# Two 3x3 convolutions re-laid: row taps in the partitions, column phase in the free dimension, copies by DMA in groups, half matmuls for half-zero weights, and one layer-norm step moved to VectorE

## The reference, cut to what matters

```python
q = ln(q.reshape(B_, E, L).transpose(0, 2, 1), gq, bq)   # the same for k and v
...
y = xr + conv3(jax.nn.gelu(conv3(xr, c1w, c1b), approximate=False), c2w, c2b)
x = x + y            # x of the sum is the input; xr comes from the normalised image
```

## Time and profile before

| | |
|---|---|
| median of 3 runs | 831.84 us (830.34 to 832.01) |
| the profiled execution: its own time | 833.53 us |
| its span, first to last instruction | 831.7 us |
| PE busy / DVE busy / ACT busy / POOL busy | 90% / 79% / 73% / 59% |
| granted PE clock, mean over the span | 0.995 of full speed (2.4 GHz) |

### The profile page before, as it was taken

One profiled execution on the slowest core, in us unless ns is written; L12 is line 12 of the kernel. 1 busy time (PEld: TensorE's weight loads), 2 busy tenths in 40 slices (PEclk: granted clock), 3 DMA queues, 4 the chain that ended last, 5 costly groups with the idle time before them and its releaser, 6 DMA issues.

```text
span 831.7 us, 18390 instructions
## 1 busy us (share of the span) xinstructions
PE 749.4 (90%) x5704; PEld 536.1 (64%) x5704; DVE 659.3 (79%) x2141; ACT 603.8 (73%) x1287; POOL 491.9 (59%) x1041
## 2 busy tenths in 40 slices
PE   0479999989899999999899999998989999999988
PEld 0257777767456677766656677776645677776753
DVE  5548888987868888888867888898776888887575
ACT  1388888877567888886737888877747788887840
POOL 5356776763346777765436776775335677776410
PEclk9999999999999999999999999999999999999999
DMA  7111160100112132100111216100011213000002
GB/s 256 58 30 30 31 230 5 53 2 1 58 64 90 36 120 111 58 1 1 59 39 52 71 30 230 58 2 1 7 52 65 96 30 130 0 1 1 2 1 101
DMA packets 17643, 47.00 MB, mean 57 GB/s; under 512 B 2080, under 2 KB 2720, under 8 KB 17568
## 3 DMA queue, kind: packets, MB, share of 16 engines
q1 hardware_dynamic: 17568, 46.09, 16.2%
HBM read 37.69 MB, written 8.39 MB: 55 GB/s over the span
## 4 chain that ended last, share of the span: by engine, by line
PE 46%; DVE 23%; issue 11%; POOL 10%; ACT 9%; DMA 1%; DVEq 0%; SPq 0%; ACTq 0%; POOLq 0%
PE y_ps L1011 11%; PE o_bank L1090 6%; PE s_ps L1065 4%; PE pt_ps L1078 4%; POOL ln_rs L724 4%; DVE h_lo L506 3%; DVE ln_st L542 3%; PE ox_ps L1034 3%; DVE h_hi L503 3%; PE s_ps L1124 3%; ACT qk_n L856 3%; PE ox_ps L1124 3%; PE o_bank L1124 3%; PE pt_ps L1124 3%; PE t_ps L1045 2%
## 5 line engine op out<-in xcount | busy, mean ns | idle before, releaser
L856 ACT ACTIVATE qk_n<-y_ps,ln_nr,ln_rs 128x128 f32<-128x128 f32 x256 | 103.7, 459 | 94.7 <-POOL ln_nr L727 94.0
L737 POOL TENSOR_TENSOR sc<-sc,mx 128x512 f32<-128x512 f32 x128 | 133.7, 1045 | 39.2 <-DVE mx L577 39.2
L1011 PE MATMUL y_ps<-w_hi,x_hi 128*128 128x192 f16 (+1 forms) x512 | 148.4, 290 | 0.0
L1011 PE MATMUL y_ps<-w_hi,x_lo 128*128 128x192 f16 (+1 forms) x512 | 148.1, 289 | 0.0
L1011 PE MATMUL y_ps<-w_lo,x_hi 128*128 128x192 f16 (+1 forms) x512 | 148.0, 289 | 0.0
L562 DVE TENSOR_TENSOR sc<-s_ps,biasS 128x512 f32<-128x512 f32 x128 | 86.8, 678 | 54.9 <-PE s_ps L1065 53.7
L1090 PE MATMUL o_bank<-v_bd,pt 128*128 128x66 f32 x1024 | 129.3, 269 | 0.0
L1090 PEld LDWEIGHTS o_bank<-v_bd,pt 128*128 128x128 f32 x1024 | 125.2, 193 | 0.2
L542 DVE BATCH_NORM_STATS2 ln_st<-y_ps 128x6 f32<-128x128 f32 x384 | 88.9, 287 | 42.9 <-PE y_ps L1011 41.1
L720 POOL TENSOR_TENSOR ln_ve<-ln_mv,eps_y 128x3 f32<-128x3 f32 x128 | 33.8, 264 | 148.2 <-DVE ln_mv L547 148.0
L724 POOL TENSOR_TENSOR ln_rs<-ln_ve,neg_half 128x3 f32<-128x3 f32 x128 | 113.3, 885 | 10.7
(11 more groups left out here) (181 smaller groups left out, 1612.4 us busy)
## 6 DMA issues: line engine op xcount, KB each, us to landing
xs<-in_x_sh_dram SPq DMA_DIRECT2D x32, 576.0 KB, 4.2
xst<-in_x_al_dram SPq DMA_DIRECT2D x16, 512.0 KB, 8.0
xf<-in_x_al_dram SPq DMA_DIRECT2D x32, 256.0 KB, 5.3
out_dram<-xf SPq DMA_DIRECT2D x32, 256.0 KB, 2.0
wst<-in_wqkv_dram SPq DMA_DIRECT2D x1, 768.0 KB, 4.2
w1s<-in_w_dram SPq DMA_DIRECT2D x1, 256.0 KB, 8.8
w2s<-in_w_dram SPq DMA_DIRECT2D x1, 256.0 KB, 8.8
biasS<-in_bias_t_dram SPq DMA_DIRECT2D x1, 256.0 KB, 9.7
```

The lines of the kernel that those rows point to most:

```text
L737: pool.tensor_tensor(sc[i % 4][:, :, :, :], sc[i % 4][:, :, :, :], mx[i % 2][:, :, :].unsqueeze(2).to_broadcast([P, HP, TOK, 2]), ALU.subt ...
L856: ins = act.activation(qk_n[j][:, t, :].rearrange("p (h y x) -> p h y x", h=HEADS, y=2), by_head(y_ps[j][:, E * t:E * (t + 1)]), ACT.Identity,
L1011: ins = pe.matmul(y.rearrange("p (t e) -> p t e", t=3)[:, :, cols], xx[r % 2][:, s, a % 2, 2 * TS * (a // 2):2 * TS * (a // 2 + TS)], ww[: ...
```

## The change

- The input of both convolutions now lies in one buffer `x4`: partition = (tap row `ay`, row phase, channel), so each partition group of 64 holds the image shifted by 0 or 1 row, which makes four image rows lie in the partitions; the column phase is in the free dimension. ACT, POOL and DVE write hi and lo parts into small staging buffers (`xr_st`, `h_st`), and SP copies them into `x4` with four DMAs for each group (`place_x`: 5 groups of an image, `place_h`: 7 groups).
- With this layout two of the four taps have non-zero weights for all 128 outputs, and each of the other two for only 64 of them. A tile takes 6 matmuls with 128 output columns and 6 with 64, the two halves alternating. The number of matmuls stays 12.
- `border` is gone: the staging rows carry a zero column, written once, and two memsets on the first and on the last tile's `hst` make the zero rows. The first row of `x4` is cleared after c2 tile 0.
- New order in step -4: c2 tiles 0 and 1, then c1 tiles 11 and 12 (on PE, ACT and DVE); c1 tile 11 uses another bank. DVE does `low` of tile 10 before the head.
- c1 waits for the copies (`x_in`), c2 for its groups of copies (`h_in`), `split` and `low` wait until the staging buffer they write has been copied out.
- In the layer norm the mean is negated by DVE right after the statistics, where POOL did it between variance and power.
- The host lays data and weights out to match.

The diff, cut to its core:

```diff
-        xr_hi = sb("xr_hi", [P, G + 2, G + 2], F16)
-        xr_lo = sb("xr_lo", [P, G + 2, G + 2], F16)
-        hst = [sb(f"hst{i}", [P, T1R, G + 1]) for i in range(6)]
-        h_hi = sb("h_hi", [P, G + 1, G + 1], F16)
-        h_lo = sb("h_lo", [P, G + 1, G + 1], F16)
+        xr_st = [sb(f"xr_st{i}", [P, 2, 2 * TS, G + 2], F16) for i in range(2)]
+        hst = [sb(f"hst{i}", [P, T1R, G + 2]) for i in range(6)]
+        h_st = [sb(f"h_st{i}", [P, 2, 2 * T1R, G + 2], F16) for i in range(3)]
+        x4 = sb("x4", [P, 2, 2, G + 1, G + 2], F16)
...
-        c1_bank = [t_bank if t == 10 else c_ps[t % 2 if t < 4 else (t + 2) % 4] for t in range(T1N)]
+        c1_bank = [c_ps[t % 2 if t < 4 else (t + 2) % 4] for t in range(10)] + [t_bank, o_bank[:, :], c_ps[2]]
         pt_bank = pt_ps[:, :, :].rearrange("p h n -> p (h n)")
-        c2_bank = [c_ps[3], c_ps[2], pt_bank, o_bank[:, :], ox_ps[:, :], pt_bank, o_bank[:, :], ox_ps[:, :]]
+        c2_bank = [c_ps[3], pt_bank, c_ps[2], o_bank[:, :], ox_ps[:, :], pt_bank, o_bank[:, :], ox_ps[:, :]]
...
-        BORDER1 = 10
+        H_GROUPS = ((0, 2), (2, 4), (4, 6), (6, 8), (8, 10), (10, 11), (11, 13))
+        H_OF = [next(g for g, (t0, t1) in enumerate(H_GROUPS) if t0 <= t < t1) for t in range(T1N)]
+        C1_LATE = -4
...
+            def place_x(b, r0, r1):
+
+                sp.wait_ge(xr_split, b * NROW + r1)
+                n = (r1 - r0) * TS * (G + 2)
+                at = TS * (r0 % 2) * (G + 2)
+                for px in range(2):
+                    src = xr_st[r0 // 2 % 2][64 * px:64 * px + 64, :, :, :].rearrange("p l i j -> p l (i j)")
+                    for ay in range(2):
+                        dst = x4[64 * ay:64 * ay + 64, :, px, :, :].rearrange("p l i j -> p l (i j)")
+                        to = (TS * r0 + 1 - ay) * (G + 2)
+                        sp.dma_start(dst[:, :, to:to + n], src[:, :, at:at + n]).then_inc(
+                            x_in[2 if r0 == NROW - 1 else r0 // 2 % 2], 16)
+
+            def place_h(b, g):
+
+                t0, t1 = H_GROUPS[g]
+                n = b * len(H_GROUPS) + g
+                sp.wait_ge(h_split, b * T1N + t1)
+                for px in range(2):
+                    src = h_st[n % 3][64 * px:64 * px + 64, :, :, :].rearrange("p l i j -> p l (i j)")
+                    for ay in range(2):
+                        dst = x4[64 * ay:64 * ay + 64, :, px, :, :].rearrange("p l i j -> p l (i j)")
+                        i0 = 1 if g == 0 and ay == 1 else 0
+                        k = (T1R * (t1 - t0) - i0) * (G + 2)
+                        to = (T1R * t0 + i0 - ay) * (G + 2)
+                        sp.dma_start(dst[:, :, to:to + k], src[:, :, i0 * (G + 2):i0 * (G + 2) + k]).then_inc(
+                            h_in[n % 3], 16)
...
-                    for r in range(4):
+                    for r in range(2):
                         row(b + 1, r)
+                for r in (0, 2, 4):
+                    place_x(b, r, r + 2)
+                place_x(b, 6, 7)
+                for g in range(3):
+                    place_h(b, g)
+                if followed:
+                    for r in range(2, 4):
+                        row(b + 1, r)
+                place_x(b, 7, 8)
+                for g in range(3, len(H_GROUPS)):
+                    place_h(b, g)
...
             def low(b, t):
 
-                rows = slice(T1R * t, T1R * (t + 1))
+                n = b * len(H_GROUPS) + H_OF[t]
+                t0 = T1R * (t - H_GROUPS[H_OF[t]][0])
+                hs = [h_st[n % 3][:, l, t0:t0 + T1R, :] for l in range(2)]
                 v.wait_ge(gelu_done, b * T1N + (t + 1))
-                v.tensor_scalar(h_hi[:, rows, :], hst[t % 6][:, :, :], up[:, 1:2], None, ALU.mult).then_inc(
-                    h_hi_done, 1)
+                if t in (0, T1N - 1):
+                    py, edge = (1, 0) if t == 0 else (0, T1R - 1)
+                    for px in range(2):
+                        q = 64 * px + 32 * py
+                        ins = v.memset(hst[t % 6][q:q + 32, edge:edge + 1, :], 0.0)
+                    ins.then_inc(h_rows, 1)
+                    v.wait_ge(h_rows, b * 2 + (1 if t == 0 else 2))
+                if n >= 3:
+                    v.wait_ge(h_in[n % 3], 64 * (n // 3))
+                v.tensor_scalar(hs[0], hst[t % 6][:, :, :], up[:, 1:2], None, ALU.mult).then_inc(h_hi_done, 1)
                 v.wait_ge(h_hi_done, b * T1N + (t + 1))
-                v.scalar_tensor_tensor(h_lo[:, rows, :], hst[t % 6][:, :, :], up[:, 1:2], h_hi[:, rows, :],
-                                       ALU.mult, ALU.subtract).then_inc(h_split, 1)
-
-            def border(b, done, zeros):
...
-                    for t in range(BORDER1, T1N):
-                        low(last, t)
-                    border(last, T1N, 2)
+                    v.wait_ge(ln_moments, p0 + (m + 1))
+                    v.tensor_scalar(ln_nm[m % 2][:, :], ln_mv[m % 2][:, :, 0], -1.0, None, ALU.mult).then_inc(
+                        ln_negated, 1)
                 if last is not None:
                     for t in result_in.get(i, ()):
                         sum_input(last, t)
                         result(last, t)
...
+                if t == 0:
+                    v.memset(x4[0:32, :, :, 0:1, :], 0.0).then_inc(x_edge, 1)
...
                 low(b, 9)
-                border(b, BORDER1, 1)
+                low(b, 10)
                 if followed:
                     head(b + 1, step, b)
                 else:
-                    for t in range(BORDER1, T1N):
+                    sum_input(b, 0)
+                    result(b, 0)
+                    for t in range(11, T1N):
                         low(b, t)
-                    border(b, T1N, 2)
-                    for t in range(T2N):
+                    for t in range(1, T2N):
                         sum_input(b, t)
                         result(b, t)
...
-            for t in (xr_hi, xr_lo):
-                for k in (0, G + 1):
-                    pool.memset(t[:, k:k + 1, :], 0.0)
-                    ins = pool.memset(t[:, 1:G + 1, k:k + 1], 0.0)
+            for t in xr_st:
+                pool.memset(t[:, :, :, :], 0.0)
+            for t in hst:
+                pool.memset(t[:, :, G + 1:G + 2], 0.0)
+            for k in (0, G):
+                ins = pool.memset(x4[:, :, :, k:k + 1, :], 0.0)
...
-                rows = slice(TS * r + 1, TS * (r + 1) + 1)
-                pool.tensor_tensor(xr_lo[:, rows, 1:G + 1], xr[:, TS * r:TS * (r + 1), :], xr_hi[:, rows, 1:G + 1],
-                                   ALU.subtract).then_inc(xr_split, 1)
+                at = TS * (r % 2)
+                hi, lo = (xr_st[r // 2 % 2][:, l, at:at + TS, 1:G + 1] for l in range(2))
+                pool.tensor_tensor(lo, xr[:, TS * r:TS * (r + 1), :], hi, ALU.subtract).then_inc(xr_split, 1)
...
-                    pool.tensor_tensor(ln_ve[j][:, :], ln_mv[j][:, :, 1], eps_y[:, :], ALU.add)
-                    pool.tensor_scalar(ln_nm[j][:, :], ln_mv[j][:, :, 0], -1.0, None, ALU.mult).then_inc(
+                    pool.tensor_tensor(ln_ve[j][:, :], ln_mv[j][:, :, 1], eps_y[:, :], ALU.add).then_inc(
                         ln_var_eps, 1)
                     pool.wait_ge(ln_var_eps, p0 + (m + 1))
                     pool.tensor_tensor(ln_rs[j][:, :], ln_ve[j][:, :], neg_half[:, 0:3], ALU.pow).then_inc(
                         ln_pow, 1)
                     pool.wait_ge(ln_pow, p0 + (m + 1))
+                    pool.wait_ge(ln_negated, p0 + (m + 1))
                     pool.tensor_tensor(ln_nr[j][:, :], ln_nm[j][:, :], ln_rs[j][:, :], ALU.mult).then_inc(
...
-                act.activation(xr_hi[:, TS * r + 1:TS * (r + 1) + 1, 1:G + 1], xr[:, TS * r:TS * (r + 1), :],
+                if r // 2 in (0, 1) and b > 0:
+                    act.wait_ge(x_in[r // 2], 128 * b)
+                    if r // 2 == 1:
+                        act.wait_ge(x_in[2], 64 * b)
+                elif r // 2 > 1:
+                    act.wait_ge(x_in[r // 2 % 2], 128 * b + 64)
+                at = TS * (r % 2)
+                act.activation(xr_st[r // 2 % 2][:, 0, at:at + TS, 1:G + 1], xr[:, TS * r:TS * (r + 1), :],
                                ACT.Copy).then_inc(xr_hi_done, 1)
...
+                if last is not None and i == C1_LATE:
+                    for t in range(11, T1N):
+                        c1_out(last, t)
+                    act.activation(wait_exp[:, :], vec[:, 0:1], ACT.Exp)
...
-                pe.wait_ge(xr_split, b * NROW + min((T1R * (t + 1) - 1) // TS, NROW - 1) + 1)
+                k = min((T1R * (t + 1) - 1) // TS, NROW - 1)
+                pe.wait_ge(x_in[0], 128 * b + (64 if k < 4 else 128))
+                if k >= 2:
+                    pe.wait_ge(x_in[1], 128 * b + (64 if k < 6 else 128))
+                if k == NROW - 1:
+                    pe.wait_ge(x_in[2], 64 * (b + 1))
+                if t == 0 and b > 0:
+                    pe.wait_ge(x_edge, b)
...
```

(70 more changed lines are left out.)

57 lines of the change are left out of this document (25 added, 32 removed).

## The result

The changed kernel takes 884.05 us (median, 882.11 to 885.55), the kernel before 831.40 on the same chip: a ratio of 1.063 [1.0605, 1.0662], 52.6 us slower. I had forecast 26 us faster. The profile shows parts that gained and parts that lost, so I go by cause. Two executions of single_rows and one of loads_late, further down, ran in a slower state and stand in the medians given there; without them these are 832.8 and 826.4.

The account below looks back on a forecast made before the run. PE was taken as the main bound, with a path through DVE, POOL and ACT in the loop. Three cycles of 6.4 (19.1), the last image's 1.7 and the tail's 5.3 made 26.1 us: 807.4 profiled, 806 median, range 791 to 824.

Parts of the forecast that it names:

- What bounds the kernel: PE in the head and tail; in the steady loop a path through DVE, POOL and ACT too; DVE at an image's end.
- Halved taps: Convolution tiles: two half matmuls share PE's array, 9 slots for 12, less 0.25 us a tile for switching.
- Rival (a): In the convolution tiles the halves run one after the other: 839 us; chance 0.14 together with (b).
- Rival (b): In the convolution tiles the halves' weight loads are not hidden: 830 to 842 us; chance 0.14 together with (a).
- Negation: Layer norm, ln_ve to power: 0.23 us saved a pass, 1.5 an image taken, 1.0 given back by DVE.
- Rival (d): DVE becomes the bound in the loop, the negation's term turns to -1.5: 818 us; chance 0.18 together with (c).
- End of image: PE from c1 tile 10 to conv(1): 10.6 us instead of 13.8, gain 3.2, copies late by 0 to 0.5.
- border wait: End of an image: PE's first c2 matmul no longer waits 1.50 us for DVE's border memsets.
- DVE's low and the buffers of h: End of an image: DVE's low of tile 10 waits for group 2's copies, with 1 us to spare.
- Tail: After the last pair's last projection: 23.9 us instead of 29.25, a gain of 5.3.
- Rival (c): Copies replace the border wait at an image's end: 3 to 5 us an image, 818 to 826; chance 0.18 with (d).
- steady loop: Four pairs in the loop take 17.8 to 18.1 us, against 18.20 before.

Follow-up runs that it names:

- single_rows: The changed kernel with each row of windows of x copied by itself, with its own semaphore, 8 groups an image instead of 5: 833.57 us.
- loads_late: As single_rows, with the next image's loads of rows 2 and 3 issued after the last copy of x: 826.54 us.
- h4: As loads_late, with four staging buffers for h instead of three: 812.38 us, 0.977 of the kernel before.
- h4_full: As h4, with the half-zero taps multiplied over all 128 outputs, so 12 full matmuls a tile: 824.41 us.
- copies_once: The changed kernel with the copies of x made for the first image only: 828.65 us.
- warm: The changed kernel with unused matmuls ahead of the waits of c1 tile 0 (30) and tile 11 (18): 873.47 us.

## Why the prediction was wrong

The forecast was 806, 26 us faster; measured was 884. The step that failed is the check of the copies against their readers: it was not made for c1 tiles 0 and 3, and for tile 11 it had issue and landing too short. By the prediction's own steps:

- **What bounds the kernel: right**, and it stayed so in h4. In after, SP's queue and the copies joined.
- **Halved taps: right in size.** c1 1.69 to 1.52 (measured 1.47 to 1.49 at the higher clock), c2 2.63 to 2.22 (2.18). Entry, exit and late second half came to 0.2 a tile for the 0.25 taken. Their worth on the path was too high: 12 us by h4_full for 17, with a part of the difference lost to the clock. Rival (a), halves one after the other, did not happen: pairs are 0.23 apart. Rival (b), loads that aren't hidden, did not happen either: six halves with six loads take 0.77 us. The rule of the Trainium skill that I had set beside it (TensorE: Matmul & The Clock Gate, Part 3, The mechanism: loads overlap only where the row groups differ) disagrees with the trace for halves as it did for full tiles; the measurement decides.
- **Negation: right in kind, too small.** 4.4 and 7.2 us by two experiments, against 3.0 after what I let DVE give back (6.0 without that). Rival (d), DVE as the bound, did not happen.
- **End of image: failed in the copies.** The border wait went as said. In its place stands the wait of c1 tile 11, 4.6 us in this period (17.7 in the four images) where I had 0 to 0.5. PE arrives as computed, 4.9 us after POOL's last split (4.7 forecast). The copies arrive 9.5 after it, not 4.0 to 5.0: queue 1.05, issues 0.69 us each and not 0.48, landing 5.7 us after the last issue and not 2 to 3. I had taken the landing from a stretch with two loads alone; here copies of h and the next image's loads run beside them, 245 GB/s in all at the end of the wait.
- **The step that failed outright: c1 tiles 0 and 3.** I checked the copies for tile 11, for c2, for ACT's splits and for DVE's buffers, and wrote "issued three steps, 13 us, earlier: nothing" for ACT's. For the first tiles of c1 I did no such sum. A group of two rows makes them wait for a row that they do not read. The rows were there, in the trace of the kernel before (POOL's split of row 1, and c1 tile 0):

```profile
374.69 1.13 POOL L709 TENSOR_TENSOR xr_lo<-xr,xr_hi 128x512 f16<-128x512 f32 x1 [2.40 <-ACT xr_hi L805]
```

```profile
375.48 0.30 PE L980 MATMUL y_ps<-xr_hi,w_hi 128*128 128x325 f16 x1
```

PE began the tile before row 1 was split. With the split's end at 375.8, my 2 us for four issues and the 4.3 of the earlier trace rows the data are there at 382.1: 6.6 us of waiting (measured 7.4). Tiles 0 and 3 hold 40.5 of the 62.9 us of c1's waits, and splitting the groups gave 50.5 us.
- **DVE's low and the buffers of h:** "1 us to spare" for group 2, which tile 10 needs, was nearly right (0.4 and 0.9 us of waiting). I did no such sum for tile 11, which needs group 3, and its copies stand on SP behind the last row of x and the loads. In the changed kernel that is hidden, since PE and the Gelu of tile 11 are late; when they came earlier (loads_late) DVE waited 7.2 and 7.9 us for it in the second and third image, and a fourth buffer was worth 14.2 us.
- **The clock: not in the sum.** I had PE near 1.00 throughout. Waits of 7.4 and 4.6 us were followed by 1.2 GHz. Filling them gave back 10.6 us by experiment.
- **Tail: 23.9 forecast, 27.3 measured** (end of the last projection, 853.2, to 880.5). In h4 it is 24.2. The chain of the changed kernel there is SP's: 20 issues of 0.63 from 846.1 to 858.7, then the landing, for which tile 11 waits 2.28 us:

```profile
858.78 2.88 DMA x<-xr_st
```

- **Rival (c)**, the copies in the place of the border wait, was the right mechanism at tile 11, priced at 3 to 5 us an image with 818 to 826 for it. The copies cost 18.5 an image, because they hold up tiles 0 and 3 as well and bring the low clock with them.

The rest of the forecast holds when the copies are out of the way: 810.2 (copies_once, for four images) and 812.4 (h4) against 806. The steady loop of the changed kernel, four pairs from scores to scores, is 17.79 us:

```profile
503.52 0.71 PE L1133 MATMUL s_ps<-k_m,q_m 64*128 64x128 f32 x8
...
521.31 0.71 PE L1133 MATMUL s_ps<-k_m,q_m 64*128 64x128 f32 x8
```

17.8 to 18.1 was forecast.

What stays open: what the clock costs in all (10.6 us by warm, 16 by the rows named, 20.8 by PE's busy time), the rest of the 5 us between the halves' terms and h4_full (up to the last image 3.7 of it is clock), and why the fourth buffer is worth 14.2 us with the copies of x and nothing without them.
